# Expert work of a 16-sequence transformer kernel in blocks of 256 rows, with the weights held still in the matmul array and one step per place

## The reference

```python
for l in range(L):                       # L = 4, 16 heads, 4 key/value heads of 64
    res = x
    h = _rms(x, ln1_w[l])
    h = _attention(h, wq[l], wk[l], wv[l], wo[l], cos, sin, causal_bias)
    x = jnp.clip(res + h, -100.0, 100.0)
    res = x
    h = _rms(x, ln2_w[l])
    h = _moe(h, wr[l], wg[l], wu[l], wd[l])
    x = jnp.clip(res + h, -100.0, 100.0)

def _moe(x, wr, wg, wu, wd):             # E = 8 experts, FF = 256
    probs = jax.nn.softmax(x @ wr, axis=-1)
    topv, topi = jax.lax.top_k(probs, 2)
    topv = topv / jnp.sum(topv, axis=-1, keepdims=True)
    comb = jnp.sum(jax.nn.one_hot(topi, E, dtype=x.dtype) * topv[..., None], axis=-2)
    for e in range(E):
        h = jax.nn.silu(x @ wg[e]) * (x @ wu[e])
        out = out + comb[..., e:e + 1] * (h @ wd[e])
```

## Time and profile before

| what | value |
|---|---|
| median of 3 runs | 3354.49 us (3334.46, 3354.49, 3355.78) |
| the profiled execution | 3336.53 us, of which the span of instructions is 3334.7 us |
| granted TensorE clock over the span | 0.91 of full speed |
| PE, DVE, ACT, POOL busy | 2653.1, 2285.3, 2001.3, 1860.3 us |
| DMA | 511.54 MB, 153 GB/s over the span |

### The profile page before, as it was taken

The page is one execution under the profiler, slowest core; times in us unless marked ns, Lnnn a source line. Parts: engine busy times, 40 slices in busy tenths (PEclk is TensorE's granted clock), DMA queues, the critical chain, the costliest instruction groups (busy, mean ns, idle before and its releaser), DMA issues.

```text
span 3334.7 us, 66162 instructions
## 1 busy us (share of the span) xinstructions
PE 2653.1 (80%) x20406; PEld 2128.6 (64%) x20406; DVE 2285.3 (69%) x8164; ACT 2001.3 (60%) x7080; POOL 1860.3 (56%) x1662
## 2 busy tenths in 40 slices
PE   5317888999789977988789977988789977989572
PEld 2216666777577765777677766776677766777462
DVE  6786766677776777766776677767776677766343
ACT  3017776776666766666666666666666665666320
POOL 0026776555766576556665575555765575555403
PEclk9659999999999999999899998999999998999665
DMA  9211222664266624553275524553266524552574
GB/s 367 117 46 64 79 89 89 209 212 137 74 207 213 203 79 152 186 179 117 80 234 199 181 83 155 188 174 111 93 217 202 183 74 141 177 183 93 173 249 127
DMA packets 287021, 511.54 MB, mean 153 GB/s; under 512 B 39968, under 2 KB 159296, under 8 KB 286144
## 3 DMA queue, kind: packets, MB, share of 16 engines
q1 hardware_dynamic: 270288, 473.72, 41.8%
q0 software_dynamic: 16384, 33.59, 3.2%
HBM read 316.58 MB, written 106.69 MB: 127 GB/s over the span
## 4 chain that ended last, share of the span: by engine, by line
PE 35%; DVE 29%; ACT 14%; POOL 13%; issue 5%; DMA 2%; SPq 2%; DVEq 0%; POOLq 0%
ACT arena L1055 6%; PE psum L784 6%; PE psum L759 5%; POOL arena L1308 4%; PE psum L802 4%; DVE arena L1572 4%; DVE arena L1593 4%; POOL arena L1275 3%; DVE arena L1563 3%; ACT arena L1063 2%; POOL rows_in L1299 2%; DVE arena L1591 2%; PE psum L804 2%; PE psum L902 2%; PE psum L832 2%
## 5 line engine op out<-in xcount | busy, mean ns | idle before, releaser
L1055 ACT ACTIVATE arena<-arena 128x128 f32<-128x128 f32 (+1 forms) x2048 | 902.3, 445 | 58.1 <-DVE arena L1597 58.1
L1308 POOL TENSOR_TENSOR arena<-arena 128x512 f32<-128x512 f32 (+1 forms) x512 | 745.3, 1475 | 238.3 <-DVE arena L1602 238.3
L1323 POOL TENSOR_TENSOR arena<-arena 128x512 f32<-128x512 f32 x320 | 401.5, 1281 | 478.1 <-DMA arena<-arena 477.9
L1063 ACT COPY arena<-psum 128x384 f32<-128x384 f32 x1024 | 446.9, 482 | 302.7 <-PE psum L784 299.7
L784 PE MATMUL psum<-arena 128*128 128x128 f32 x3072 | 479.4, 295 | 162.7 <-ACT arena L1063 108.8
L784 PEld LDWEIGHTS psum<-arena 128*128 128x128 f32 x3072 | 349.6, 147 | 286.5 <-ACT arena L1063 174.9
L759 PE MATMUL psum<-arena 64*128 64x128 f32 (+1 forms) x4096 | 451.5, 361 | 12.7 <-DVE arena L1593 6.2
L1593 DVE CUSTOM_DVE_ANT_0 arena<-psum,arena 128x256 f32<-128x256 f32 x1024 | 429.8, 420 | 0.0
L1572 DVE TENSOR_TENSOR arena<-psum,arena 128x512 f32<-128x512 f32 x640 | 392.6, 677 | 9.7 <-PE psum L834 9.7
L1055 ACT ACTIVATION_READ_ACCUMULATOR arena<-arena 128x1 f32 x2048 | 389.1, 190 | 0.0
L802 PE MATMUL psum<-arena 128*64 128x256 f32 x2048 | 339.0, 411 | 31.3 <-DVE xT_lo L1683 31.3
(11 more groups left out here) (199 smaller groups left out, 5585.2 us busy)
## 6 DMA issues: line engine op xcount, KB each, us to landing
gu<-gu_kept SPq DMA_DIRECT2D x320, 512.0 KB, 4.4
wd<-wd_kept SPq DMA_DIRECT2D x320, 256.0 KB, 4.0
arena<-arena SPq DMA_DIRECT2D x128, 384.0 KB, 3.0
arena<-arena SPq DMA_DIRECT2D x128, 256.0 KB
arena<-rows_in SPq DMA_DIRECT2D x320, 64.0 KB
rows_out<-arena SPq DMA_DIRECT2D x320, 64.0 KB, 2.5
rows_in<-arena SPq DMA_DIRECT2D x34, 512.0 KB, 8.4
rows_out<-arena SPq DMA_DIRECT2D x34, 512.0 KB, 8.2
```

Source lines behind the costliest of these rows:

```text
L1055: ins = A.activation(a, a, ACT.Exp, bias=negmax[:, q, k:k + 1], accum_out=rowsum[:, q, k:k + 1])
L1063: A.copy(probsT[:, 4 * (q % 2) + i, :], psum[:, t_bank(key), 0:3 * P]).then_inc(sem("t_free"), 1)
L1308: ins = G.tensor_tensor(a, a, r[:, :, t:t + 1].broadcast_to([P, 4, P * (t + 1)]), ALU.mult)
L1323: G.tensor_tensor(keys_and_queries(it, u), keys_and_queries(it, u), turned_part[:, u, :], ALU.add) \
```

## The change

The rows of an expert are now taken in units of 256. Both halves of a unit use the same weights, so the weights become the stationary operand and 256 rows move. The result comes out turned already: `turn_gated` is gone, and `gated`, in SBUF, is what ACT and DVE read. A batch of eight sequences has 2 x 8 + 7 = 23 units, the most that can be needed, instead of 20 steps of two tiles. One step is now whole, in one gap: PE turns the rows of unit k, multiplies unit k-2 by the down weights, and multiplies unit k-1 by the gate and up weights. It is put in gaps 0, 2, 3, 4 and 6. The gate and the up result are a `u` bank each. The last eight sequences are two batches of four with 15 units each: the first of them is worked in iterations 62 to 64 (17 gaps), the second after the loop. Weights of a unit are one array, loaded by one DMA (768 KB) into a ring of four; a third pair of tables in DRAM is added and zeroed at the start (108 DMAs of 512 KB instead of 68). In ACT's order `scale_routed` and `round_piece` now stand ahead of gap 3 instead of behind it, `exps` of quarter 3 stands whole behind gap 7, and copies of attention results stand ahead of a step's last part (`step_end`).

```diff
-NB = NIT // HB
+FIRST = [HB * b for b in range(NIT // HB)] + [NIT - 4]
+END = FIRST[1:] + [NIT]
+NB = len(FIRST)
 CAP = HB * S
-PT = 20
-HS = 2 * PT + 2
-ROWS = NE * CAP + NE * P
+UR = 2 * P
+UNITS = [2 * (b - a) + NE - 1 for a, b in zip(FIRST, END)]
+UNIT0 = [sum(UNITS[:b]) for b in range(NB + 1)]
+ROWS = NE * CAP + NE * UR
...
+def step_places():
+        last = END[b] - 1
+        places = [(last + 1 + u, p) for u, ps in ((1, (4, 6)), (2, (0, 2, 3, 4, 6)), (3, (0, 2, 3, 4, 6)), (4, (0, 2, 3, 4, 6)),
+                                                  (5, (0, 2, 3, 4, 6)), (6, (0, 2, 3))) for p in ps] if b < NB - 2 else \
+            [(NIT - 2, 4), (NIT - 2, 6)] + [(NIT - 1, p) for p in (0, 1, 2, 3, 4, 6, 7)] + [(NIT, p) for p in range(8)]
+        assert len(places) == UNITS[b] + 2
+        for k, where in enumerate(places):
+            assert where not in at
+            at[where] = (b, k)
...
+    def moe(b, k):
+        g = UNIT0[b] + k
+        if k < UNITS[b]:
+            u["rows", g] = len(u)
+        if k >= 2:
+            t["y", g - 2] = len(t)
+        if 1 <= k <= UNITS[b]:
+            u["gate", g - 1] = len(u)
+            u["up", g - 1] = len(u)
...
+            def begin(b):
+
+                for k in range(W_RING):
                     fetch(b, k)
-                if 1 <= k <= PT:
-                    fetch_down(b, k - 1)
-                if k >= 3:
-                    put_back(b, k - 3)
+
+            def after_step(b, k):
+
+                if k >= 2:
+                    put_back(b, k - 2)
+                if 2 <= k < UNITS[b] - 2:
+                    fetch(b, k + 2)
+                if k == UNITS[b] + 1 and b == NB - 3:
+                    begin(b + 1)
...
                 u_was_read(pe, ("rows", g))
-                for j in range(2):
-                    key = ("gate", g, j)
-                    u_is_free(key)
-                    o = psum[:, u_bank(key), :]
-                    hi, lo = (a[:, j * P:(j + 1) * P] for a in (xT_hi, xT_lo))
-                    T.matmul(o, hi, gu[:, g % W_RING, j, 0:2 * FF], start=True, stop=False)
-                    T.matmul(o, hi, gu[:, g % W_RING, j, 2 * FF:4 * FF], start=False, stop=False)
-                    T.matmul(o, lo, gu[:, g % W_RING, j, 0:2 * FF], start=False, stop=True).then_inc(sem("u_full"), 1)
-
+                hi, lo = (a[:, g % 2, :] for a in (xT_hi, xT_lo))
+                for m, name in enumerate(("gate", "up")):
+                    u_is_free((name, g))
                     for f in range(2):
-                        c = (2 * j + f) * P
-                        mm = T.transpose(psum[:, u_bank(("gated", g)), c:c + P],
-                                         gated[:, gate_side(g, j), f * P:(f + 1) * P], ident)
-                mm.then_inc(sem("u_full"), 1)
+                        o = psum[:, u_bank((name, g)), f * UR:(f + 1) * UR]
+                        w_h, w_l = (w_now[:, g % W_RING, k, (2 * m + f) * P:(2 * m + f + 1) * P] for k in range(2))
+                        T.matmul(o, w_h, hi, start=True, stop=False)
+                        T.matmul(o, w_h, lo, start=False, stop=False)
+                        mm = T.matmul(o, w_l, hi, start=False, stop=True)
+                    mm.then_inc(sem("u_full"), 1)
...
-            def moe(b, hs):
-                m = hs // 2
-                g = b * PT + m
-                if hs % 2 == 0:
-                    if m < PT:
-                        turn_rows(g)
-                    if m > 0:
-                        turn_gated(g - 1)
-                else:
-                    if m < PT:
-                        gate_and_up(g)
-                    if m > 0:
-                        down(g - 1)
+            def step_of(b, k):
+                g = UNIT0[b] + k
+                if k < UNITS[b]:
+                    turn_rows(g)
+                if k >= 2:
+                    down(g - 2)
+                if 1 <= k <= UNITS[b]:
+                    gate_and_up(g - 1)
...
             def round_gated(g):
-                u_is_full(act, ("gated", g))
-                A.copy(hh_hi, psum[:, u_bank(("gated", g)), :]).then_inc(sem("hh_hi_ready"), 1)
+                act.wait_ge(sem("gated_ready"), g + 1)
+                A.copy(hh_hi, gated).then_inc(sem("hh_hi_ready"), 1)
...
+            def step_of(b, k):
+                g = UNIT0[b] + k
+                if k < UNITS[b]:
+                    round_rows(g)
+                if k >= 2:
+                    copy_y(g - 2)
+                if 1 <= k <= UNITS[b]:
+                    open_gate(g - 1)
+
+            def step_end(b, k):
+                if 1 <= k <= UNITS[b]:
+                    round_gated(UNIT0[b] + k - 1)
...
             def gate(g):
                 dve.wait_ge(sem("th_ready"), g + 1)
-                b = S_RING + T_RING
-                step(V.scalar_tensor_tensor(opened, th, 1.0, psum[:, b:b + 2, 0:FF], ALU.add, ALU.mult))
-                V.tensor_tensor(gated, opened, psum[:, b:b + 2, FF:2 * FF], ALU.mult).then_inc(sem("u_free"), 2)
+                V.scalar_tensor_tensor(flat(opened), flat(th), 1.0, psum[:, u_bank(("gate", g)), :], ALU.add, ALU.mult) \
+                    .then_inc(sem("u_free"), 1)
+                u_is_full(dve, ("up", g))
+                u_was_read(dve, ("gate", g))
+                V.tensor_tensor(flat(gated), flat(opened), psum[:, u_bank(("up", g)), :], ALU.mult).then_inc(sem("u_free"), 1)
+                u_was_read(dve, ("up", g))
+                V.memset(done_flags[:, 4:5], 0.0).then_inc(sem("gated_ready"), 1)
 
             def low_gated(g):
                 dve.wait_ge(sem("hh_hi_ready"), g + 1)
-                V.tensor_tensor(hh_lo, psum[:, u_bank(("gated", g)), :], hh_hi.bitcast(F32), ALU.subtract) \
-                    .then_inc(sem("u_free"), 1)
-
-            def moe(b, hs):
-                m = hs // 2
-                g = b * PT + m
-                if hs % 2 == 0:
-                    if m < PT:
-                        low_rows(g)
-                    if m > 0:
-                        low_gated(g - 1)
-                elif m < PT:
-                    gate(g)
+                V.tensor_tensor(hh_lo, gated, hh_hi.bitcast(F32), ALU.subtract).then_inc(sem("hh_lo_ready"), 1)
+
+            def step_of(b, k):
+                g = UNIT0[b] + k
+                if k < UNITS[b]:
+                    low_rows(g)
+                if 1 <= k <= UNITS[b]:
+                    gate(g - 1)
+
+            def step_end(b, k):
+                if 1 <= k <= UNITS[b]:
+                    low_gated(UNIT0[b] + k - 1)
```

More of the change, by code:

```diff
@@ L478, in pieces_stored @@
         def pieces_stored(n):
-            return sum(64 if is_expert(it) else 32 for it in PIECES[:n])
+            return 32 * n
         def stored_before(it):
@@ L1198, in _ @@
                     copy_h(it + 1)
[L1199 to L1200 removed]
+                place_end(it, 2)
                 if old:
```

345 lines of the change are left out of this document (151 added, 194 removed).

## The result

The changed kernel takes 3630.03 us (median of 4 runs, 3627.63 to 3645.28) against 3355.14 for the kernel before in the same job: ratio 1.0845, 95% interval 1.0794 to 1.0896. The prediction was 3450, at most 3580: slower was right, the size was not. The profiled execution has a span of 3643.5 us, 308.8 more than the one of before, where the prediction's sum gave 105. It is the slowest of the four, 15 us above their median, and the one of before was 19 us under its median; between the medians the difference is 275.

A forecast was written before the change was run, and what follows sets the result against it. Bound: PE's own order, plus a stall and lower clock with gathers. Iteration 44.6 + 8.6 + 1.8 + 0.8 = 55.8 us; loop +136, end -31, so 3336.5 + 105 = 3442, plus 8: 3450 us; 8-in-10 range 3290 to 3580.

The forecast's parts named there:

- The stall that goes: Gap 1: PE's wait behind DVE's adding of gathered rows, with its low clock, goes; 5.1 us per gathering iteration.
- the bare 44.5: Iteration with expert work but no gathers, in the first layer before the change: 44.5 us, the forecast's starting point.
- PE's work, +1.1 us an iteration: Expert steps on PE: five of 2.98 us replace four of 3.44, adding 1.1 us an iteration.
- The wait that it adds, 8.6 us: Gaps 2, 3, 4, 6 and 0: PE's up matmul waits for `low_rows` of rows just turned; 8.6 us an iteration.
- the sentence on gap 4: Gap 4: PE has 4.6 us of work before up, DVE 5.6 including `low_gated` and `low_rows`; wait 1.0 us.
- The clock, 1.8 us: After gap 3's wait PE runs at the lower clock: 1.8 us more an iteration, bounds 0 and 5.6.
- Two SBUF operands, 0.8 us: `low_gated` on DVE reads two SBUF operands and may meet GpSimd: 0.8 us an iteration, bounds 0 and 2.1.
- The light ends, -12.3 us a batch: A batch's first and last gaps, lacking some work and waits with 23 units in 25 gaps: 12.3 us less.
- The end, -31 us: Iterations 62 to 64 cost +60 us, the steps after the loop gain 71, fewer final gathers gain 20.
- Slower still: Rival: lower clock after two waits an iteration and the full port cost; 59.5 us an iteration, 3580 us; chance 0.11.
- The waits hide: Rival, faster: only gaps 2 and 6 or so wait, 3.5 to 4.5 us; iteration 49, 3210 us; chance 0.16.
- The end does not shorten: Rival: DMA latency keeps steps after the loop at 7.75 us, 132 instead of 84, 3500 us; chance 0.03.

The follow-up runs named there:

- before_combine_late: Kernel before the change, with DVE's `combine` moved behind `copy_o` and also behind `place(it, 1)`: 3236.4 us, ratio 0.967.
- apart_down_last: Changed kernel with turned rows last in a step and in the scores' ring of four banks, and gate and up ahead of `down`: 3359.7 us, ratio 1.007.
- apart_down_end: apart_down_last with `round_gated` and `low_gated` directly behind the step's other instructions in all gaps: 3479.2 us, ratio 1.043.
- end3_first: Changed kernel with gap 3's `round_gated` and `low_gated` moved ahead of `copy_routed` (ACT) and rope's products (DVE): 3622.3 us, ratio 1.081.
- adl_end3: apart_down_last with gap 3's `round_gated` and `low_gated` moved ahead of `copy_routed` and rope's products: 3332.3 us, ratio 0.995.
- order_only: Changed kernel with each step ordered down, gate and up, turned rows, the rows still in the expert ring of two banks: 3672.9 us, ratio 1.101.
- end_at_once: Changed kernel with `round_gated` and `low_gated` directly behind the step's other instructions in all gaps: 3602.9 us, ratio 1.077.
- ring_only: Changed kernel with turned rows in the scores' ring of four banks, the order in a step unchanged: 3568.8 us, ratio 1.068.
- rows_apart: Changed kernel with turned rows in the scores' ring of four banks and last in each step, behind down and gate and up: 3510.5 us, ratio 1.050.
- before_copy_first: Kernel before the change, with DVE's `copy_o` ahead of `combine` in gap 1: 3274.4 us, ratio 0.979.

## Why the prediction was wrong in size

**The stall that goes.** Right in kind: no wait stands behind `combine`, and gathering iterations cost the same as others. Its size, 5.1 us, was 3.7 by before_combine_late, where gathering iterations stay 1.1 us above the others. This changes nothing in the sum for the changed kernel, which was made from the bare 44.5.

**PE's work, +1.1 us an iteration.** Near, 1.6 by this count: in a stretch of apart_down_last at full clock PE is busy for 47.0 us with 411 matmuls, which is 44.3 for the 387 of an iteration; before it was 42.7 for 354 at full clock. The windows (53 us of apart_down_last, then 45 of the kernel before):

```profile
1489.00:1542.00 53.00, 47.02 (x411) 40.44 (x411) 42.03 (x154) 34.97 (x121) 29.29 (x26) 1.00 0.40 137
```

```profile
670.00:715.00 45.00, 42.66 (x354) 35.16 (x353) 31.40 (x124) 32.59 (x115) 23.79 (x22) 1.00 0.61 200
```

**The wait that it adds, 8.6 us.** The sum was near, the account was not. Forecast by gap against the trace: gap 2 2.0, 1.83; gap 6 1.5, 1.07; gap 0 1.3, 0.72; gap 3 2.8 for `xT_lo`, 1.42 for hh_lo; gap 4 1.0 for `xT_lo`, 2.57 for hh_lo. Together 7.6. (Gap 0's 1.3 is a slip of the sum, 10.0 less 8.8 is 1.2.) The failed step is the sentence on gap 4, which has `low_gated` in DVE's chain but lets PE wait only at `up`. `down` of that unit comes before, and its operand is what `low_gated` writes: PE is there 0.22 + 2.35 = 2.6 us after gap 3's up result, DVE 0.8 + 6 x 0.61 + 0.7 = 5.2. The difference is 2.6, and the trace has 2.57. I listed who waits for `low_rows` and never asked who waits for `low_gated`, though the code says so in the first line of `down`.

**The clock, 1.8 us.** Under-sized: with 47.95 us busy for 388 matmuls against 44.3, the lower clock costs 3.7 an iteration, in this one in two falls, both behind waits for hh_lo. The whole iteration is 44.3 of work at full clock, 3.7 of clock, 7.6 of waits for the two operands, 1.7 of the wait in `attend` and 0.7 of small ones: 58.0. Of the 2.2 over the forecast 55.8 the clock is 1.9; the wait in `attend` was not in the sum, and 1.0 of the waits that were did not come.

**Two SBUF operands, 0.8 us.** `low_gated` takes 782 ns on the mean of 191 and 693 in the stage where GpSimd has no tensor work: 0.1 each, 0.5 an iteration. The Trainium skill, "SBUF — State Buffer", section "SBUF: two separate sides", would have such an instruction and GpSimd's lock each other out for a whole one, and by the prediction's pricing each would have cost 0.5. The trace agrees with the rule and not with the pricing, which let every `low_gated` meet a product of GpSimd. All 35 that took over 0.8 us began while such a product was running, and ended 0.55 us after it did; the 156 others have a mean of 0.68. It is the same with 49 of them in apart_down_last and 66 in apart_down_end. One of the 35 and the products of GpSimd beside it, which end at 1494.19:

```profile
1493.49 1.25 DVE L1677 TENSOR_TENSOR hh_lo<-arena,hh_hi 128x512 fp32r<-128x512 f32 x1
...
1491.29 2.90 POOL L1284 TENSOR_TENSOR arena<-arena 128x512 f32<-128x512 f32 x2 [8.72 <-DVE arena L1577]
```

**The light ends, -12.3 us a batch.** Measured -4.9 in the second batch shown (285.0 against 5 x 58.0 = 290). It looks as if taking a gap's work out did not take its wait out, and the wait moved to the next gap as in end3_first; no run tested this. With the iteration this makes 19 us a batch, 113 in the six batches and 26 in the first.

**The end, -31 us.** Iterations 62 to 64 were +78 for +60. The final steps fell by 42 instead of 71: 7.2 us each, where I counted DVE's chain alone, 3.6, and `finish`. The chain is longer by PE's gate, up and down, all of it at a granted clock of 0.65, since `down` waits for hh_lo there too (30 us in these steps). That transfers did not set it is shown by apart_down_last, 5.2 us a step with the same transfers, at a DMA share of 0.67 instead of 0.43; how its gain is shared between the order and the clock that came with it is not shown, since adl_end3, in the same order at the lower clock, takes 6.9. The gathers, -18.5 for -20, were right. The end is 49 us of the miss.

Sum: 139 + 49, 11 up to the first batch and 5 between batches make the 204 us between 308.8 and 105. Of the 139, the longer iteration is 35 x 2.2 = 77, most of it the clock; the other 62 are the light ends and the first batch's iterations. So the step that failed in mechanism, the wait of `down` for hh_lo, shows in the size by way of the clock more than by the sum of waits. That sum was near by luck: three waits for `xT_lo` came out smaller than forecast, two did not come, and two for hh_lo came in their place.

**Rivals.** "Slower still", 59.5 us an iteration, was the nearest. "The waits hide" is what apart_down_last comes near: with both waits mostly gone its batches last 252 us and it takes 3360, not 3210. "The end does not shorten" named transfers as the cause; that is refuted; the steps took 113 us, between its 132 and the forecast's 84.

**What is shown and what is argued.** That the order and the ring behind the two waits cost the 8% is shown by apart_down_last, with the same work, units, transfers and split: 221 of their 329 us are gone, and 270 us of time. None of its three edits does it by itself: the ring gives 61 us, the turned rows last cost 43, gate and up ahead of `down` costs 337. That a wait moves to the other one, or to another bank, when it is hit by a single edit is shown by end3_first, order_only and, in part, end_at_once and ring_only; with ring and order together, in rows_apart, 27 of 153 us came back at hh_lo. What keeps adl_end3's batch at 249 us, where before_combine_late has 229, stays open: five steps give PE 1.1 us more and DVE's operations of a step, 2.6 us, once more, but no run separated these.

## What to carry to other kernels

For every instruction that an edit moves, list all its readers from the code, and set each reader's place in its engine's order against the time of the result; a ring of two banks that holds both an input of a step and its outputs makes the step a handshake between engines. A wait in such a chain moves when it is hit alone: remove the shared bank and cover the latency with the engine's own work together, since gate and up ahead of `down` cost 337 us with the turned rows first in a ring of two, and gained 151 with them last in a ring of four. And try the cheap repair first: the stall that this change went round was gone when `combine` was moved, for 3.3%.

## What the runs showed of the hardware

The same order of instructions can run in two rhythms, at two granted clocks, for many steps on end. The final steps of adl_end3 and apart_down_last, above, are one case: eleven intervals in a row of 6.9 us in adl_end3, a mean of 5.2 in apart_down_last. The first layer's iterations of before_copy_first and of the kernel before, where no gathered rows are added, are the other: 48.0 us and 44.9, three or more in a row. In the slower one PE has a wait of 2.0 us at L784 in each iteration, and a window behind it reads

```profile
718.00:726.00 8.00, 7.73 (x52) 6.30 (x53) 2.07 (x10) 7.37 (x29) 3.82 (x4) 0.79 0.47 161
```

with 1.00 in the five other windows of that iteration; in the kernel before, the longest wait of PE in that stretch is 1.1 us and the clock stays at 1.00. It looks as if PE's lateness at the lower clock makes the next wait, and that the next fall of the clock; this was not tested. It is worth 3 us of 45, and 19 us over eleven of the final steps, so a difference of a per cent between two orders need not be what the order costs by itself.
